# Layer 1's mixture: first product transposed with weights loaded per group, results stored by the sync engine; layer 1's blocks in five column pieces

## The reference

```python
def gcn_conv(x, src, dst, W, b, n):
    h = x @ W
    ...
    return jax.ops.segment_sum(h[src] * norm[:, None], dst, num_segments=n) + b
...
gate_logits = x @ gate_w + gate_b                 # 16 experts
topk_vals, topk_idx = jax.lax.top_k(gate_logits, 2)
topk_w = softmax(topk_vals)
h = relu(einsum('bsh,ehf->bsef', x, w1) + b1)     # 256 -> 512
expert_out = einsum('bsef,efh->bseh', h, w2) + b2 # 512 -> 256
moe = sum(topk_w[..., None] * take(expert_out, topk_idx), axis=2)
y = x + moe;  return layer_norm(y) * gamma + beta
```

## Time and profile before

| | us |
|---|---|
| median of 3 runs (lowest, highest) | 4691.11 (4682.94, 4698.04) |
| the profiled execution, its own time | 4690.25 |
| its span, first to last instruction | 4688.5 |
| PE, DVE, POOL, ACT busy | 2993.0, 2362.7, 2467.4, 538.1 |

### The profile page before, as it was taken

How to read it: one execution, slowest core, us unless ns; L and a number is a source line. 1 busy time by engine, 2 the same in 40 slices (tenths; PEclk the granted TensorE clock), 3 DMA queues, 4 the chain that set the end, 5 groups by cost and what they waited for, 6 DMA issues and landing times. The chain is left out here.

```text
span 4688.5 us, 48107 instructions
## 1 busy us (share of the span) xinstructions
PE 2993.0 (64%) x14109; PEld 2196.6 (47%) x14110; DVE 2362.7 (50%) x4967; ACT 538.1 (11%) x1489; POOL 2467.4 (53%) x1832
## 2 busy tenths in 40 slices
PE   3121417520499997248822999996979488883793
PEld 2111205410499987225512888885534133333552
DVE  6897896950399987312226334313243255452004
ACT  1000111100000000101103010002320011111120
POOL 2578777777254656676673000067774277772003
PEclk9555767855699999579966999996989655565896
DMA  9762222211799997556642333330013333333232
GB/s 359 282 208 36 32 23 36 40 10 0 268 387 383 335 316 247 142 116 133 131 122 56 134 136 137 137 112 16 2 51 120 111 105 104 105 104 70 74 112 64
DMA packets 351060, 627.69 MB, mean 134 GB/s; under 512 B 175337, under 2 KB 271436, under 8 KB 324801
## 3 DMA queue, kind: packets, MB, share of 16 engines
q1 hardware_dynamic: 149525, 437.74, 26.5%
q0 software_dynamic: 171920, 118.57, 14.3%
q10 hardware_dynamic: 29456, 69.37, 3.9%
HBM read 475.91 MB, written 148.85 MB: 133 GB/s over the span
## 5 line engine op out<-in xcount | busy, mean ns | idle before, releaser
L772 POOL DMA_INDIRECT weight_cells<-added_weight,added_row x391 | 670.2, 1714 | 507.7 <-DMA weight_cells<-added_weight,added_row 233.1
L447 POOL DMA_INDIRECT count_cells<-cells_count,added_row x391 | 713.8, 1826 | 329.3 <-issue 121.8
L1386 PE MATMUL g_acc<-XN,g_blocks 125*125 125x128 f32 x5000 | 567.4, 275 | 277.7 <-DMA g_blocks<-count_cells 268.0
L1615 POOL DMA_INDIRECT slots_dram<-sort_rec,sort_row x392 | 389.4, 993 | 646.1 <-DVE sort_row L1604 515.0
L1386 PEld LDWEIGHTS g_acc<-XN,g_blocks 125*125 125x125 f32 x5000 | 559.2, 189 | 282.6 <-issue 268.2
L1702 PE MATMUL g_acc<-g_H,g_blocks 125*125 125x256 f32 x2500 | 549.9, 380 | 19.7 <-DMA g_blocks<-weight_cells 19.2
L830 PE MATMUL g3g_pp<-g3g_got,g3g_hot 128*125 128x256 f32 x832 | 443.6, 641 | 135.8 <-DMA g3g_got<-relations,g3g_idx 81.0
L817 POOL DMA_INDIRECT g3g_got<-relations,g3g_idx x416 | 394.6, 948 | 255.6 <-ACT g3g_idx L810 134.0
L1702 PEld LDWEIGHTS g_acc<-g_H,g_blocks 125*125 125x125 f32 x2500 | 470.5, 188 | 91.4 <-issue 19.6
L634 DVE SCALAR_TENSOR_TENSOR same_product<-same_window,cells_id,same_earlier 128x1024 bf16<-128x1024 f32 x392 | 489.7, 1280 | 2.9 <-ACTq L93 0.6
L1457 DVE SCALAR_TENSOR_TENSOR g_product<-g_ids,cells_id,g_weights 128x1024 bf16<-128x1024 f32 x392 | 480.6, 1281 | 7.8
(11 more groups left out here) (570 smaller groups left out, 4150.9 us busy)
## 6 DMA issues: line engine op xcount, KB each, us to landing
g_blocks<-count_cells SPq DMA_DIRECT2D x100, 1562.5 KB, 11.2
g_blocks<-weight_cells SPq DMA_DIRECT2D x50, 1562.5 KB, 6.5
count_cells<-edges_stripe POOLq DMA_DIRECT2D x25, 1562.5 KB, 42.9
weight_cells<-edges_stripe ACTq DMA_DIRECT2D x25, 1562.5 KB, 41.1
same_window<-ids_dram SPq DMA_DIRECT2D x49, 512.0 KB, 3.8
g_ids<-ids_dram SPq DMA_DIRECT2D x49, 512.0 KB, 4.6
g_weights<-weights_dram SPq DMA_DIRECT2D x49, 512.0 KB, 7.1
relations<-g_ys SPq DMA_DIRECT2D x25, 1000.0 KB
```

Of the source, the lines that this page charges most:

```text
L447: pool.indirect_dma_start(out=rows, out_offset=bass.IndirectOffsetOnAxis(ap=g.cell_row[:, t:t + 1], axis=0), in_=g.cell_count[:, t:t + 1], ...
L772: pool.indirect_dma_start(out=rows, out_offset=bass.IndirectOffsetOnAxis(ap=g.cell_row[:, t:t + 1], axis=0), in_=g.cell_weight[:, t:t + 1] ...
L1386: last = nc.tensor.matmul(acc[0:P, i % ACCS, 0:128], blocks[0:P, i % BLOCKS, t * P:(t + 1) * P], rhs[p][:, t, :], start=(t == 0), stop=(t ...
L1615: pool.indirect_dma_start(out=g.slots_dram[:, :], out_offset=bass.IndirectOffsetOnAxis(ap=self.row[:, c:c + 1], axis=0), in_=self.rec[:, c ...
```

## The change

1. The constants: EARLY_WINDOWS from 27 to 33, MIDDLE_WINDOWS from 46 to 47.
2. In layer 1's graph layer each block is loaded by five DMAs of 625 columns (2500 bytes per row) in place of one of 3125; PE still waits for all of them.
3. In the mixture's first stage ACT loads w2 alone (four DMAs of 2 MB), and b1 turned, one number per hidden column: 8192 runs of 4 bytes in one DMA.
4. w1 is loaded per slot by SP, 512 KB, four places, four slots ahead.
5. The first product has w1 stationary and xT moving, 8 matmuls of 128 columns in place of 2 of 512. So h comes out transposed: DVE's addition of b1, the four transposes, and pU are gone. ACT adds b1 and takes the relu in four pieces of 128x128 right out of pH, with the bias of the slot's expert.
6. SP stores the results, and its b1 broadcast (256 KB per slot) is gone. ACT reads kmap in each body, PE reads it once, not twice. The merged results Y lie in w2's room, not w1's.

The diff, cut to its core:

```diff
-EARLY_WINDOWS, MIDDLE_WINDOWS = 27, 46
+EARLY_WINDOWS, MIDDLE_WINDOWS = 33, 47
+PIECE = N // 5
@@ layer1_gnn, sync, tensor
-                sp.dma_start(blocks[:, i % BLOCKS, :], g.count_cells[j * 128:(j + 1) * 128, :]).then_inc(loaded[i % BLOCKS], 16)
+                for c in range(0, N, PIECE):
+                    sp.dma_start(blocks[:, i % BLOCKS, c:c + PIECE],
+                                 g.count_cells[j * 128:(j + 1) * 128, c:c + PIECE]).then_inc(loaded[i % BLOCKS], 16)
-                        pe.wait_ge(loaded[i % BLOCKS], 16 * (i // BLOCKS + 1))
+                        pe.wait_ge(loaded[i % BLOCKS], 16 * (N // PIECE) * (i // BLOCKS + 1))
@@ layer1_ffn, first stage, scalar
                 for c in range(EXPERT_LOADS):
-                    for load in expert_loads(nc, g, a, c):
-                        load(act)
+                    act.dma_start(g.w2[:, :].rearrange("p (c k n) -> p c k n", c=EXPERT_LOADS, n=D)[:, c],
+                                  a["L1_ffn_w2"][c * n:(c + 1) * n].rearrange("e (k p) n -> p (e k) n", p=128)).then_inc(g.w_loaded, 16)
+                    act.dma_start(b1[:, :, :], a["L1_ffn_b1"].rearrange("e (f p) -> p e f", p=128)).then_inc(b1_loaded, 16)
@@ the loop over the slots, sync
+                def load_hidden(e, j):
+                    sp.dma_start(w1[:, j, :, :], a["L1_ffn_w1"][bass.ds(e, 1)].rearrange("a (k p) n -> p (a k) n", p=128)
+                                 ).then_inc(w1_loaded[j], 16)
+                for j in range(AHEAD):
+                    load_hidden(e[j], j)
+                    load_bias(e[j], j)
                 sp.wait_ge(scattered, done)
                 for j in range(AHEAD):
                     load_rows(j, j)
-                    load_bias(e[j], j)
...
                         sp.wait_ge(x_turned, n + 1)
                         load_rows(n + AHEAD, j)
+                        sp.wait_ge(h_made, n + 1)
+                        load_hidden(e[j], j)
                         sp.wait_ge(y_put, n + 3)
+                        sp.dma_start(results[bass.ds(n, 1)].rearrange("a p d -> (a p) d"), ys[:, j % 2, :]).then_inc(stored[j % 2], 16)
                         load_bias(e[j], j)
@@ tensor
                     pe.wait_ge(x_read, n + 1)
-                    for k in range(K2):
-                        last = nc.tensor.matmul(pH[:, j % 2, :], xT[:, j % 2, k * 128:(k + 1) * 128],
-                                                w1f[:, bass.ds(expert * (K2 * F) + k * F, F)],
-                                                start=(k == 0), stop=(k == K2 - 1))
+                    for f in range(KF):
+                        for k in range(K2):
+                            last = nc.tensor.matmul(pH[:, j % 2, f * 128:(f + 1) * 128],
+                                                    w1[:, j % AHEAD, k, f * 128:(f + 1) * 128],
+                                                    xT[:, j % 2, k * 128:(k + 1) * 128],
+                                                    start=(k == 0), stop=(k == K2 - 1))
...
-                        pe.wait_ge(h_put, n + 1)
-                        for k in range(KF):
-                            last = nc.tensor.transpose(pU[:, j % 2, k * 128:(k + 1) * 128], h[:, j % 2, k * 128:(k + 1) * 128], g.ident[:, :])
-                        last.then_inc(h_turned, 1)
@@ scalar
-                        act.wait_ge(h_turned, n + 1)
-                        nc.scalar.activation(hT[:, j % 2, :], pU[:, j % 2, :], ACT.Relu).then_inc(h_read, 1)
+                        act.wait_ge(h_made, n + 1)
+                        for f in range(KF):
+                            last = nc.scalar.activation(hT[:, j % 2, f * 128:(f + 1) * 128], pH[:, j % 2, f * 128:(f + 1) * 128],
+                                                        ACT.Relu, bias=row(b1, expert[j], f, f + 1, p=128))
+                        last.then_inc(h_read, 1)
                         read_rows(n + 2, j)
-                        act.wait_ge(y_put, n + 3)
-                        act.dma_start(results[bass.ds(n, 1)].rearrange("a p d -> (a p) d"), ys[:, j % 2, :]).then_inc(stored[j % 2], 16)
@@ vector
-                        put_hidden(n + 1, i + (1 if j + 1 < AHEAD else 2), (j + 1) % AHEAD)
```

More of the change, by code:

```diff
@@ L1946, in _ @@
             def _(act):
+                n = NE // EXPERT_LOADS
                 for c in range(EXPERT_LOADS):
-                    for load in expert_loads(nc, g, a, c):
-                        load(act)
+                    act.dma_start(g.w2[:, :].rearrange("p (c k n) -> p c k n", c=EXPERT_LOADS, n=D)[:, c],
+                                  a["L1_ffn_w2"][c * n:(c + 1) * n].rearrange("e (k p) n -> p (e k) n", p=128)).then_inc(g.w_loaded, 16)
+                with nc.allow_non_contiguous_dma("a bias per column of the hidden layer"):
+                    act.dma_start(b1[:, :, :], a["L1_ffn_b1"].rearrange("e (f p) -> p e f", p=128)).then_inc(b1_loaded, 16)
         gate(nc, g, "f1g", a["L1_ffn_gate_w"], a["L1_ffn_gate_b"], NE, logits)
@@ L1998, in take @@
                 return room[:, used - width * places:used].rearrange("p (j d) -> p j d", j=places)
-            xs, xT, ys, h, hT = take(D, AHEAD), take(D), take(D), take(F), take(F)
-            pT, pH, pU, pY = (ps1(m, [128, 2, 512]) for m in ("pT", "pH", "pU", "pY"))
-            x_loaded, b_loaded = ([sem1(f"{m}{j}") for j in range(AHEAD)] for m in ("x_loaded", "b_loaded"))
+            xs, xT, ys, hT = take(D, AHEAD), take(D), take(D), take(F)
+            pT, pH, pY = (ps1(m, [128, 2, 512]) for m in ("pT", "pH", "pY"))
+            x_loaded, b_loaded, w1_loaded = ([sem1(f"{m}{j}") for j in range(AHEAD)] for m in ("x_loaded", "b_loaded", "w1_loaded"))
             stored = [sem1(f"stored{j}") for j in range(2)]
-            x_turned, x_read, h_made, h_put, h_turned, h_read, y_made, y_put = (
-                sem1(m) for m in ("x_turned", "x_read", "h_made", "h_put", "h_turned", "h_read", "y_made", "y_put"))
+            x_turned, x_read, h_made, h_read, y_made, y_put = (
+                sem1(m) for m in ("x_turned", "x_read", "h_made", "h_read", "y_made", "y_put"))
             bins = g.bins.rearrange("(s p) d -> s p d", p=128)
@@ L2032, in _ @@
                         load_rows(n + AHEAD, j)
+                        sp.wait_ge(h_made, n + 1)
+                        load_hidden(e[j], j)
                         sp.wait_ge(y_put, n + 3)
+                        sp.dma_start(results[bass.ds(n, 1)].rearrange("a p d -> (a p) d"), ys[:, j % 2, :]).then_inc(stored[j % 2], 16)
                         load_bias(e[j], j)
+                for j in range(2):
+                    sp.wait_ge(stored[j], 16 * (SLOTS // 2 + 1))
                 for j in range(AHEAD):
                     sp.wait_ge(x_loaded[j], 16 * (BODIES + 1))
-                    sp.wait_ge(b_loaded[j], 32 * (BODIES + 1))
+                    sp.wait_ge(b_loaded[j], 16 * (BODIES + 1))
+                    sp.wait_ge(w1_loaded[j], 16 * (BODIES + 1))
             @block.tensor
@@ L2117, in _ @@
                         n = AHEAD * i + j
-                        put_hidden(n + 1, i + (1 if j + 1 < AHEAD else 2), (j + 1) % AHEAD)
+                        dve.wait_ge(b_loaded[j], (i + 1) * 16)
                         dve.wait_ge(stored[j % 2], (2 * i + j // 2 + 1) * 16)
                         dve.wait_ge(y_made, n + 1)
-                        nc.vector.tensor_tensor(ys[:, j % 2, :], pY[:, j % 2, 0:D], b[:, j, F:F + D], ALU.add).then_inc(y_put, 1)
+                        nc.vector.tensor_tensor(ys[:, j % 2, :], pY[:, j % 2, 0:D], b[:, j, :], ALU.add).then_inc(y_put, 1)
         with ExitStack() as sub:
             sb1, ps1, sem1 = bufs(nc, sub, "f1y")
-            Y = [g.w1[:, k * T * D:(k + 1) * T * D].rearrange("p (t d) -> p t d", t=T) for k in range(2)]
+            Y = [g.w2[:, k * T * D:(k + 1) * T * D].rearrange("p (t d) -> p t d", t=T) for k in range(2)]
             C = T // G
```

32 lines of the change are left out of this document (13 added, 19 removed).

## The result

| | us |
|---|---|
| before, median of 6 runs (lowest, highest) | 4693.4 (4682.94, 4699.85) |
| after, median of 6 runs (lowest, highest) | 4678.34 (4675.13, 4680.71) |
| ratio, 95% interval | 0.9963 (0.9952 to 0.9973) |
| span of after's profiled execution | 4673.4 (before 4688.5) |

The change gains 15 us where 80 were forecast. Faster, as said, but 68 us above the forecast and outside the range.

The account below looks back on a forecast made before the run. Layer 1 was taken as bound by PE in the graph layer, the sort before the scatter, then PE and POOL tied in the loop. Scatter -16, loop -65.6, pieces +2: 4690.25 - 80 = 4610 us, range 4590 to 4660.

Parts of the forecast that it names:

- POOL's windows: In layer 1's graph layer, each POOL window of eight additions takes 21.4 us, so POOL is ready to scatter at 1947.
- POOL late: Rival ahead of layer 1's scatter: windows take 23 us or more, scatter at 1980, time 4643 us; chance 0.15.
- The loop: In layer 1's loop, a PE slot falls from 4.96 to 3.95 us; with its start, 65.6 us saved.
- dear product: Rival in the loop: first product's weight loads add to its columns, 3.5 us, slot 5.68, time 4720; chance 0.02.
- DMA-bound loop: Rival in the loop: DMA bounds it, share 1.11, slot 4.38 us, time 4637 us; chance 0.12.
- DMA share near 1: Sign that the forecast is wrong: a DMA share near 1 in the loop, where 0.90 was forecast.
- The weights: In the mixture's first stage, loads take 15 us (12 to 20), the gate starts some 20 us earlier, posi at 1943.
- The pieces: In layer 1's graph layer, blocks loaded in five DMAs cost up to +13 us at 359 GB/s; +2 taken.

## Why the prediction was wrong

**The step that failed** is the windows' price, under "POOL's windows". It had the bounds right (19.75 quiet, 23.0 full, 27.1 old) and took the middle, 21.4, on the ground that the last two passes leave the queue emptier. They hardly do. The third and the fourth pass after (columns as in the earlier trace rows):

```profile
1526.00:1663.00 137.00, 137.00 (x1164) 130.69 (x1164) 123.08 (x230) 5.68 (x21) 86.68 (x47) 0.98 1.04 343
1663.00:1800.00 137.00, 124.31 (x1060) 120.97 (x1060) 119.29 (x218) 5.51 (x20) 88.02 (x46) 0.95 0.97 310
```

With a DMA share of 1.04 and 0.97 the wait stays near 6 us until 1800 and is 5.7 on the mean of all 25 windows. Eight issues without a wait are 19.75 - 2.15 = 17.6 us; with 5.7, and with three pauses of POOL of 4.4 to 5.5 us inside windows, which no single window of the earlier trace rows showed and which come to 0.6 per window, that is 23.9. Measured are 23.8. So 25 windows were done at 1851 where 27.6 should have been. The rival "POOL late" was this case. Its scatter for windows of 24 us, 1999, was near; its time for them, 4662, was too low, since behind the scatter it let the loop bind, as the forecast did.

**Ahead of the scatter**: 2.6 windows more at the forecast's own 17.0 us are 44, and the store of the table took 13; the other seven windows behind 1851 cost what the forecast took for them (122 us). The store was in the trace of before, but there it met the scatter and no additions; the forecast moved POOL's work beside it without pricing that. POOL was ready at 2003.5, not 1947: +56.5.

**Behind the loop**: 14 windows took 269.1 us where 261.8 were taken (+7.3), and the pause behind the table's reload was new (+14.6). The 9.3 us that POOL had to spare against the gathers are used up. 56.5 + 7.3 + 14.6 - 9.3 = 69 us: gathers at 2364.7 against 2295.6. The result is 68 above the forecast.

**The loop** was right and even cautious: 251.4 us against 267.7, the row transposes at their lower bound (0.22), the second product at 1.73, not 1.80, no wait for ACT (L2082 has no idle time), and no edge of the body. The first product's 1.79 against 1.77 refutes "dear product". The Trainium skill's rule (TensorE: Matmul & The Clock Gate, Back-to-back issue gap), by which it would have been 4765 us, isn't borne out either: 16 passes in 1.79 us are 0.112 each, against 0.43 for 512 columns, which is the same per column and not 2.5 times as much. The DMA-bound loop is refuted by PE, busy for 200 of 200 us; but the share was 0.96, not 0.90, so it fitted more barely than forecast, and "DMA share near 1" was no sign that it binds. None of it counted: POOL was in its last window until 2350.1, 15 us after the loop's end. **The weights**: ACT was held 5 us longer than forecast, and posi came 2 us later. That posi is so near is in part luck: counted from POOL's first addition it came 13 us earlier than before, not 20. **The pieces**: at 359 GB/s, 5.9 us per block against 5.48 would be 21 us over 50 blocks, not 13; nothing hangs on it, as PE waited for no block after the first.

**The structure of the sum** held: the later of posi and POOL starts the scatter, the later of the loop and POOL the gathers. What was wrong are the sizes of POOL's terms, and two that stood at nothing: the store beside a window, and the pauses. POOL's work from 1256 to the gathers can be added up by itself: 25 x 23.8 + 8 x 19.0 + 76 (scatter) + 269 (14 windows) + 16 (the pauses around them) = 1108 us, so 2364. The price of 23.0 alone would not have made POOL bind at the gathers: POOL would be ready at 1980 + 78 + 262 = 2320, the forecast's loop over at 2327.6 (the 4643 of "POOL late").

## What to carry to other kernels

Where an engine has a fixed list of work that spans several stages, add the list up from its first to its last item, pauses included, beside the price of each stage: a stage that gets shorter gives this engine less cover, and makes its items dearer if it moves its bytes in less time. The edits are worth little apart. By the medians and with the old split, the pieces alone gave +1 us, the mixture alone +18, both together +18; with the new split, the mixture without the pieces gave +43. All three gave -15, and -86 once the list was spread over the idle time too. When work is moved, look at what else is on the DMA queue at its new time, not only at the engine.

## What the runs showed of the hardware

- A store or load of 125 partitions by 25600 bytes moves at 128 GB/s on five engines, 0.96 us per row. POOL's additions, 4 bytes each, get one packet per row there: a window of 17 us becomes 30. Cut at 112 rows, the reload moves at 270 GB/s, and at the store the wait is 3.43 us, not 15.61.
- POOL pauses without a reason that the profile shows, and at the same places of its list. In the kernels with 33 and 47 and all windows, the indirect DMAs number 502, 555, 562, 622, 682, 745, 816, 866 and 868 are slow or late by 3 to 7 us, the last by up to 14.7 where the table's rows are on their way. Beside blocks in one piece the ones at 555 and 562 are 8 to 12 us. With other lists the numbers behind the first change move (697 and 768 with 27 early windows). What it is stays open; it costs 0.6 us per window in the graph layer.
- One DMA of 8192 runs of 4 bytes, behind 8 MB on its queue, held ACT for 5.98 us; the four 2 MB ahead of it for 14.38.
